# TensorE's order in an attention loop: both key tiles' weighted values as one group behind the second head's scores, and the shift behind the first head

## The reference

```python
scores = jnp.einsum('bhqd,bhkd->bhqk', q, k) / jnp.sqrt(jnp.float32(DK))
scores = jnp.where(mask[:, None, :, :] == 0, jnp.float32(-1000000000.0), scores)
p_attn = jax.nn.softmax(scores, axis=-1)
x = jnp.einsum('bhqk,bhkd->bhqd', p_attn, v)
```

## Time and profile before

| | |
|---|---|
| median of three runs | 263.34 us (263.17 to 263.64) |
| the profiled execution, whole | 263.62 us |
| its span, from the first instruction to the last | 261.8 us |
| outside the span | 1.8 us |
| mean granted TensorE clock, share of full speed | 0.905 |
| instructions | 4575 |
| TensorE, matmuls | 198.6 us busy |
| VectorE | 195.1 us busy |
| ScalarE | 136.6 us busy |
| GpSimd | 119.6 us busy |

### The profile page before, as it was taken

One profiled execution on the slowest core, in us unless ns is written; L12 is line 12 of the kernel. 1 busy time (PEld: TensorE's weight loads), 2 busy tenths in 40 slices (PEclk: granted clock), 3 DMA queues, 4 the chain that ended last, 5 costly groups with the idle time before them and its releaser, 6 DMA issues.

```text
span 261.8 us, 4575 instructions
## 1 busy us (share of the span) xinstructions
PE 198.6 (76%) x1646; PEld 129.2 (49%) x1646; DVE 195.1 (75%) x452; ACT 136.6 (52%) x272; POOL 119.6 (46%) x226
## 2 busy tenths in 40 slices
PE   0288596699833857728799998999996996999960
PEld 0067465489831236616344353444554883757420
DVE  6899796788567596944977768786935636679996
ACT  1256731394948657703477757876887256351000
POOL 2799553899664967770034876537004020000000
PEclk9999886779995559968979999999999999999995
DMA  5970040000400000000000000000000000000000
GB/s 162 405 314 4 0 156 5 3 0 4 160 3 0 1 0 0 3 5 3 0 0 0 4 1 4 0 3 0 0 4 3 0 3 0 4 0 20 23 20 20
DMA packets 3805, 8.72 MB, mean 33 GB/s; under 512 B 434, under 2 KB 2242, under 8 KB 3394
## 3 DMA queue, kind: packets, MB, share of 16 engines
q1 hardware_dynamic: 3312, 7.69, 8.0%
q10 hardware_dynamic: 468, 0.70, 0.8%
HBM read 7.86 MB, written 0.52 MB: 32 GB/s over the span
## 4 chain that ended last, share of the span: by engine, by line
PE 36%; DVE 34%; POOL 12%; ACT 7%; issue 6%; DMA 2%; SPq 1%; POOLq 0%; DVEq 0%
PE ps L1157 33%; DVE picksum L1122 5%; PE ps L1166 3%; POOL rstd L362 3%; DVE gate_pt L1116 3%; POOL w L374 3%; DVE rden L856 3%; DVE qd_mem L835 3%; DMA cst<-consts_dram 2%; DVE rows L784 2%; DVE mx L1010 2%; DVE gate_pt L953 2%; DVE amax L947 2%; ACT gate_pt L731 2%; DVE half_c L1000 1%
## 5 line engine op out<-in xcount | busy, mean ns | idle before, releaser
L1010 DVE TENSOR_REDUCE mx<-ps 128x2 f32<-128x512 f32 x64 | 42.3, 687 | 12.7 <-PE ps L1157 12.5
L731 ACT ACTIVATE gate_pt<-ps 128x512 f32<-128x512 f32 x64 | 37.1, 603 | 15.5 <-PE ps L1157 15.3
L504 POOL TENSOR_SCALAR gate_pt<-ka 32x256 f16<-32x256 f16 x64 | 25.5, 399 | 4.4
L1157 PE MATMUL ps<-gate_pt,half_c 128*128 128x512 f16 x64 | 25.0, 394 | 1.8 <-DVE mx L1010 0.9
L1157 PE MATMUL ps<-qb,gate_pt 128*128 128x256 f16 x128 | 25.3, 281 | 0.9
L491 POOL TENSOR_SCALAR spread<-mx 128x16 f16<-128x16 f32 x32 | 5.9, 202 | 36.5 <-DVE mx L1010 24.8
L1157 PE MATMUL ps<-gate_pt,hid_xm 128*32 128x256 f32 x256 | 20.4, 391 | 1.5 <-ACT gate_pt L731 1.5
L1157 PE MATMUL ps<-w,half_c 128*128 128x512 f16 x96 | 21.2, 380 | 0.0
L1157 PEld LDWEIGHTS ps<-qb,gate_pt 128*128 128x128 f16 x128 | 9.4, 99 | 18.8 <-issue 10.2
L1166 PE MATMUL ps<-cst,rows 128*128 128x128 f32 x32 | 7.6, 335 | 14.0 <-ACT rows L636 8.5
L362 POOL TENSOR_TENSOR rstd<-vareps,halfs 128x2 f32<-128x2 f32 x24 | 17.1, 713 | 2.0
(11 more groups left out here) (219 smaller groups left out, 544.7 us busy)
## 6 DMA issues: line engine op xcount, KB each, us to landing
stage<-weights_dram SPq DMA_DIRECT2D x2, 1024.0 KB, 7.3
wf<-weights_dram SPq DMA_DIRECT2D x4, 256.0 KB, 7.8
wf<-mask_dram SPq DMA_DIRECT2D x1, 1024.0 KB, 4.8
eb_oT<-ffw_dram SPq DMA_DIRECT2D x1, 768.0 KB, 7.8
ctx_in<-ctx_rows_dram ACTq DMA_DIRECT2D x1, 512.0 KB, 4.2
x_in<-x_dram SPq DMA_DIRECT2D x4, 128.0 KB, 4.9
gate_pt<-ctx_cols_dram SPq DMA_DIRECT2D x1, 512.0 KB, 8.1
out_dram<-ctx_in SPq DMA_DIRECT2D x4, 128.0 KB, 1.7
```

The costliest lines, as they stand in the source:

```text
L504: ins = nc.gpsimd.tensor_scalar(kz[part, n % KRING, k], ka[part, b, quad], 1.0, 0.0, ALU.mult, ALU.add)
L731: nc_act(pt[:, head % PRING].rearrange("p t n -> p (t n)"), ps[:, 2 + head % 2, :], ACT.Exp, scale=DK ** -0.5).then_inc(sig["probs"], 1)
L1010: V.tensor_reduce(mx[:, b, head:head + 2, t], score_bank(4 * n + i).rearrange("p (h n) -> p h n", h=2), AX.X, ALU.max).then_inc(sig["smax" ...
L1157: return nc.tensor.matmul(dst, lhsT, rhs, start=start, stop=stop, skip_group_check=True)
```

## The change

In the loop of `attention`, `shift(n + 1)` is issued at k = 0 instead of k = 1: behind `scores(n + 2, 0)` and ahead of that head's tail step. `weighted_values(n - 1, 0)` leaves k = 0 and is issued at k = 1, directly ahead of `weighted_values(n - 1, 1)`. Nothing is changed on the other engines.

```diff
                         if n + 2 < B * QUADS:
                             scores(n + 2, k, masked)
-                        if k == 1 and n + 1 < B * QUADS:
+                        if k == 0 and n + 1 < B * QUADS:
                             shift(n + 1)
                         if tail_at(n, k):
                             tail_step(*tail_at(n, k))
                         if (n, k) in ONEHOT_AT:
                             onehot_columns(*ONEHOT_AT[n, k])
-                        if k < TILES and n >= 1:
-                            weighted_values(n - 1, k)
+                        if k == 1 and n >= 1:
+                            for t in range(TILES):
+                                weighted_values(n - 1, t)
```

## The result

The changed kernel takes 270.26 us, the median of four runs (269.28 to 272.32), against 263.49 us for the kernel before (four runs, 263.17 to 264.14). The ratio is 1.0267, with a 95% interval of 1.0212 to 1.0321: slower. The prediction was 270.9 us in a range of 267.0 to 274.5.

The account below looks back on a forecast made before the run. The loop was taken to go at TensorE's pace and that of the waits it runs into. Terms 4.64 + 2.80 + 0.16 = 7.60 us, added to the 263.34 median, gave 270.9 us, range 267.0 to 274.5.

Parts of the forecast that it names:

- The mechanism: Shift behind the first head: TensorE gets there at 146.19, spread is ready at 146.87, so TensorE idles 0.83 us.
- Plain quads: Quads 0 to 5, 9 and 13: 0.83 us of waiting against 0.25 saved, 0.58 more each, 4.64 in all.
- Quads 6, 10 and 14: Tail transposes at the first head now stand behind the waiting shift: 0.95 us in quad 10, 0.90 in 14, sum 2.80.
- Quads 7, 8, 11 and 12: First-head tail step already makes TensorE wait, and the shift sits in that wait: four quads together cost 0.16 us.
- Quad 15: Last quad of the loop: no shift, weighted values off ScalarE's way, so no cost.
- the step from GpSimd to TensorE: Delay from spread done to shift start: 0.15 us, bounds zero and 0.3, giving 5.3 to 9.9 us in all.
- The group: Both key tiles of weighted values back to back: 0.57 + 0.43 = 1.00 us to the next start.
- The clock: TensorE in the loop: new idle gaps endanger full clock by the skill's rule, not by the last stretch; full clock kept.
- Rival 1: TensorE's clock falls in the loop, some 3.1 us per half-clock quad, one to three quads: 274 to 280; chance 0.09.
- Rival 2: Spread comes in time at the shift, only the saving is left: 3.5 us off, 259.8; chance 0.04.
- Rival 3: Part of the wait is hidden in longer quads or the tail's quads: half the sum, 267.1; chance 0.08.
- rival 4: Wait at the shift and saving cancel, with a wait of 0.25 instead of 0.83: 263.3; chance 0.02.

Follow-up runs that it names:

- experiment 1: Kernel before with only the shift moved to k = 0, the weighted values left one key tile at k = 0 and one at k = 1: 273.36 us, ratio 1.0351.
- experiment 3: Kernel before with the shift moved to k = 0 but behind weighted values of tile 0, tile 1 staying at k = 1: 267.06 us, ratio 1.0118.
- experiment 4: Changed kernel plus a third GpSimd operation of the same size ahead of the two that write spread: 272.58 us, ratio to before 1.0369.
- experiment 6: Changed kernel with spread written by one GpSimd operation for both query tiles instead of two: 268.29 us, ratio to before 1.0188.
- experiment 5: Kernel before plus one more GpSimd operation of the same size ahead of the two that write spread: 263.82 us, ratio 1.0004.
- experiment 10: Kernel before with tile 0 then the shift at k = 1, tile 1 at k = 3, and spread written by one GpSimd operation: 259.19 us, ratio 0.9816.

## Why the prediction was right

**The mechanism** is the one forecast. The shift behind the first head stands without the work that covered VectorE's scan and GpSimd's two operations; experiments 1, 3, 4 and 6 show it by leaving out the group, giving the cover back, and making spread later and earlier; experiments 5 and 10 show that spread's readiness costs nothing where there is cover. That the total came so close (270.9 us forecast, 270.26 measured) is partly luck, as the quads show.

**Plain quads.** The forecast was 0.58 us each for quads 0 to 5, 9 and 13, 4.64 in all. Quads 2 to 5 took 0.58, 0.58, 0.52 and 0.51 more than before. Quad 0 took 0.90 (4.38 instead of 3.48; its granted clock was 0.62, and 0.64 before), quad 1 0.69, quads 9 and 13 0.39 and 0.40. The sum is 4.57.

**Quads 6, 10 and 14.** Forecast 2.80, measured 0.70, 0.82 and 0.83: 2.35. **Quads 7, 8, 11 and 12.** Forecast +0.16, measured -0.20, -0.16, -0.13 and -0.18: -0.67. **Quad 15.** Forecast 0, measured -0.05. In all 6.20 against 7.60 in the loop.

**The term that was mis-sized** is the step from GpSimd to TensorE. I took 0.15 us from VectorE's release of the output projection; the rows of the changed kernel have spread done at 150.44 and the shift at 150.49, and all fifteen shifts of this kernel and of experiments 1, 4 and 6 show 0.05 as well. The prediction says that no row shows TensorE released by this operation. For the products that is so, but the kernel before had one weight load that spread released, shown above: 132.12 + 0.37 = 132.49, and the load at 132.54. The 0.05 could have been read before the run.

Fifteen shifts times 0.10 is 1.5 us, close to the 1.40 that is missing in the loop, but it is not the whole account, for other terms were off and cancel. The eight quads priced as plain would have been 3.84 us with a step of 0.05 and took 4.57. Most of the 0.73 lies in quads 0 and 1 (0.42 and 0.21), where part of the work ran at half clock: quad 1's shift waited until 137.75, since the last scores of quad 0 took 0.63 us instead of 0.38 and the maximum of them ended late. Quads 2 and 3 took 0.10 more than the 0.48 that is left, mainly since GpSimd started 0.06 us later on spread there (the last section). Against this, the seven quads with a tail step at k = 0 came out some 0.6 us below what the smaller step alone gives. The reason shows in quads 6 and 7 of the changed kernel, here TensorE's transposes and projection, each with the next start:

```profile
159.63 0.60 PE L1166 MATMUL ps<-cst,eb_oT 128*128 128x128 f32 x4
160.07 0.38 PE L1157 MATMUL ps<-qb,gate_pt 128*128 128x256 f16 x2
164.33 0.33 PE L1157 MATMUL ps<-w,y_mem 128*128 128x128 f16 x3
164.78 0.38 PE L1157 MATMUL ps<-qb,gate_pt 128*128 128x256 f16 x2
```

The four transposes take 0.44 us to the next start (159.63 to 160.07) and the projection 0.45 (164.33 to 164.78); in the kernel before they took 0.55 (171.65 to 172.20) and 0.54 (176.57 to 177.11), with the 32-column weighted values next, and the prediction carried both over. So a change to the 32-column shape cost about 0.1 us behind scores, the shift, the four transposes and the projection, and 0.14 behind the two transposes of quad 12 (0.36 us to the next start before, 0.22 now), and the group removes one of these here too. The shift itself took 0.23 us to the next start (150.49 to 150.72), 0.02 more than I gave it.

**The group.** Forecast 1.00 us to the next start; measured 1.00.

**The clock.** The rule that the prediction cites (the Trainium skill, TensorE: Matmul & The Clock Gate, Part 1) made the gaps a danger as the prediction read it, the row of the last stretch did not, and the row held: quads 3 and 4 ran at a granted clock of 1.00 (2.4 GHz) with 3.50 and 3.49 us of matmul in 4.27 and 4.21. From quad 2 on the whole loop ran at 1.00. Rival 1 is out, except that quad 0 ran partly at half clock, as it did before the change. The half-clock piece behind the loop cost this execution some 1.6 us; what brought it on stays open. TensorE had stood idle for 1.47 us ahead of the last quad's weighted values, but it had done so in the kernel before as well, where no such piece followed.

**The other rivals.** Rival 2 asked for spread 0.8 us earlier; the wait was there in all fifteen. Rival 3 was right in one part, since quads 7, 8, 11 and 12 paid nothing, but the plain quads paid in full, and with them rivals 3 and 4 fall.

## What to carry to other kernels

When an operation is moved up in an in-order stream, ask what stood between it and its input: here 0.57 us of weighted values was worth 6 us, because it covered VectorE's scan and GpSimd's two small operations. And before a price is taken from another pair of engines, look for any wait of the right pair, weight loads included: one such row had the step that was mis-sized here. Grouping products of one shape saves a change of shape (0.24 us in a plain quad), but the saving is real only where the next instruction is ready, and it was nothing when the group stood alone. Look for the place where the engine idles in every round, and put independent work there: one tile moved into the idle time at the quad's end took 3 us off.

## What was not expected of the hardware

GpSimd does not start on spread equally soon after VectorE's fourth maximum. In the changed kernel the step is 0.08 or 0.09 us nine times in fifteen and 0.14 or 0.15 six times. The six are those in which GpSimd's last operation was a copy of keys (line 504); before the nine it was another. The length of the pause does not decide it. Two of VectorE's maxima, and GpSimd's start on spread behind the second:

```profile
145.03 0.68 DVE L1010 TENSOR_REDUCE mx<-ps 128x2 f32<-128x512 f32 x1
195.53 0.68 DVE L1010 TENSOR_REDUCE mx<-ps 128x2 f32<-128x512 f32 x1
196.30 0.37 POOL L491 TENSOR_SCALAR spread<-mx 128x16 f16<-128x16 f32 x2 [4.40 <-DVE mx L1010]
```

After 4.40 us of pause behind the previous spread it started 0.09 us after the maximum (196.21 to 196.30), and after 2.02 us behind a copy of keys 0.15 us after it (145.71 to 145.86, the row of quad 3 in the timeline of the result). Quad 4's 0.09 (149.98 to 150.07) came 0.73 us behind a split of a weight (line 382). The kernel before and experiments 1 and 6 divide in the same way, but no run changes what stands ahead of spread, so the cause is open. One GpSimd operation on 128x32 elements took 0.22 us (experiment 6) where one on 128x16 takes 0.20 (experiment 4): for these two sizes the number of operations is the price, not their elements.
